# Four attention layers on one Trainium2 core: query stores held back, batch 0's queries loaded in two halves, stack loads moved by one step

## The chip, the cores and the metric

The kernel runs on one core of one Trainium2 chip. A core has five engines that run their own instruction streams: TensorE (PE in the profile, its weight loads PEld), VectorE (DVE), ScalarE (ACT), GpSimd (POOL) and SyncE (SP). They meet through semaphores. DMA transfers are issued from SP's queue and from POOL's queue and are carried out by 16 DMA engines. The metric is the device time of one launch in microseconds (us), as the median of several runs.

## The reference

The model has four layers on x of 8 batches x 256 tokens x 256 features. Each layer is a gated cross attention to a context of the same shape, and then a gated feed forward block (dense, two mixtures of experts, and a ternary one with a convolution). Only the attention is touched:

```python
h = layernorm(x)                                   # before each sublayer
q, k, v = h @ Wq + bq, ctx @ Wk + bk, ctx @ Wv + bv  # layer 0: h, ctx, ctx themselves
scores = einsum('bhqd,bhkd->bhqk', q, k) / sqrt(16)  # 16 heads of 16; layer 0 masked
out = einsum('bhqk,bhkd->bhqd', softmax(scores), v) @ Wo + bo
x = x + tanh(g_xattn[l]) * out
```

## The kernel before, in words

**Groups and batches.** The 2048 tokens are 4 groups of 512 tokens, so group g holds batches 2g and 2g+1. `project(l)` makes keys, values and queries of a layer group by group. TensorE multiplies, ScalarE writes the high part of the result (`q_hi`, `k_hi`), and VectorE writes the low part (`q_lo`, `k_lo`), the rest that a lower precision product needs. A group's queries are 1 MB: 512 KB high, 512 KB low.

**Through DRAM.** SP stores the parts into a DRAM tensor (`qk_parts`, by `store_k` and `store_q`), and POOL loads them back by batch into `stack`, which has 4 slots and holds heads in the layout that the scores need. `load_stack(l, b, at)` has four steps for a batch: `at` 0 and 1 are the keys of the two halves of the partitions, 2 and 3 the queries. Each step is two DMAs, of 128 KB (line 629) and of 256 KB (line 630). A small load of ones (line 622) comes with `at` 0 of the first four batches. `q_parts` has two buffers, so group 2 waits until group 0 is stored, and group 3 for group 1 (`stored(q_out, l, g - 2)`). The buffers of the keys lie in slot 3 of the stack.

**The attention loop.** `attend(l)` handles 256 (batch, head) units as 32 quads of 4 score pairs ("units" in this text: one PSUM bank, 2 matmuls at line 992). So a batch has 4 quads, and batch b begins at quad 4b. In quad n TensorE does, in this order: the scores of units 4n and 4n+1 (line 992) with the second scores, of units 13 earlier (line 996); a transpose of the maxima of quad n-1 (`max_rows`, line 1010); units 4n+2 and 4n+3; and the product with the values of quad n-4 (`times_v`, line 1037). VectorE takes the maximum of each unit (line 2092), ScalarE copies the transposed maxima (line 1526), and POOL writes them by DMA as a row into the stack (`put_rows`, line 667). The second scores of quad n need its row and are first due in quad n+3. ScalarE takes the exponentials (line 1517). At the first unit of a batch TensorE waits until every load of that batch has landed (`stack_in`):

```python
if c == 0 and h == 0:
    loads = sum(x % SLOTS == b % SLOTS for x in range(B)) * l + b // SLOTS + 1
    pe.wait_ge(stack_in[b % SLOTS], 128 * loads + 16 * (l + 1))
```

**POOL's order.** POOL issues the loads of batch 0, then three of the four steps of batch 1. Then it goes through the quads in order: wait for the row of quad n, put it, in quads 3 to 11 of layers 1 to 3 some work on the residual (line 644), and one step of a load:

```python
for n in range(QUADS):
    put_rows(l, n)
    ...
    if (n + 7) // 4 < B:
        load_stack(l, (n + 7) // 4, (n + 3) % 4)
```

In layer 0 it also makes the masks and takes the values between (lines 688 and 692). All of this is one queue in program order. At the first unit of a layer TensorE also waits for the low parts of all four groups of queries (line 964).

## Time and profile before

| | us |
|---|---|
| median of 3 runs | 1571.42 (1568.8 to 1572.77) |
| profiled execution, its own time | 1568.99 |
| its span | 1567.2 |
| TensorE busy | 1324.8 (85%) |
| VectorE busy | 962.4 (61%) |
| ScalarE busy | 860.1 (55%) |
| POOL busy | 708.6 (45%) |

The span is the time from the first to the last record of the profiled execution; its own time is 1.8 us more. Busy shares are means over stages with different limits, so they don't tell what bounds the stage that the change touches. "Idle before, releaser" in the rows is the time in which the engine did nothing just before an instruction, and what ended it. POOL's busy time does not count the waits of its queue.

### The profile page before, as it was taken

Reading aid. Unit: us, or ns where it says so; the run is one execution under the profiler, and the core shown is the slowest. Engines: PE = TensorE matmul, PEld = TensorE weight load, DVE = VectorE, ACT = ScalarE, POOL = GpSimd, SP = SyncE. Lnnn points to the kernel's source line nnn. Section 1 sums busy time; section 2 is a strip of 40 time slices with the busy share of each in tenths; the row PEclk is TensorE's granted clock in tenths of the full one; section 3 lists DMA queues with packets and bytes.
Section 4 is the critical chain, followed back from the end, with each engine's and each line's share of the span. In section 5 each row is a group of like instructions: output and inputs, shape, how many; then the busy total and the mean of one; then the engine's idle time right before and its main releaser. Section 6 shows DMA issues by size and latency. Waiting matters only on the chain.

```text
span 1567.2 us, 29388 instructions
## 1 busy us (share of the span) xinstructions
PE 1324.8 (85%) x9497; PEld 962.0 (61%) x9524; DVE 962.4 (61%) x2651; ACT 860.1 (55%) x1718; POOL 708.6 (45%) x835
## 2 busy tenths in 40 slices
PE   2899899997998499999999699849999388995985
PEld 1455489854566289999986366627887245664343
DVE  6789653426785643333338499575554277967787
ACT  2366854434786245555535388535554155885554
POOL 4567330105632577767641473158994415622000
PEclk9999999997899699999999699969999797997998
DMA  9997030179640333343248974024444498710001
GB/s 291 280 159 145 2 98 0 37 226 194 120 77 15 101 124 120 116 158 112 79 146 275 213 135 84 13 86 151 146 135 162 150 277 166 138 33 1 0 14 41
DMA packets 115441, 188.86 MB, mean 121 GB/s; under 512 B 21169, under 2 KB 91441, under 8 KB 109105
## 3 DMA queue, kind: packets, MB, share of 16 engines
q0 software_dynamic: 36928, 105.19, 28.2%
q1 hardware_dynamic: 78368, 81.79, 16.9%
q8 instruction: 86, 1.41, 0.4%
q14 instruction: 59, 0.48, 0.1%
HBM read 128.17 MB, written 50.20 MB: 114 GB/s over the span
## 4 chain that ended last, share of the span: by engine, by line
PE 67%; DVE 14%; DMA 7%; ACT 6%; issue 4%; POOL 1%; ACTq 0%; SPq 0%; DVEq 0%; POOLq 0%
PE PS L1196 10%; PE PS L1216 10%; PE PS L1037 9%; PE PS L992 8%; PE PS L996 3%; PE PS L1208 3%; PE PS L1074 2%; DMA qk_parts<-q_parts 2%; PE PS L1010 2%; PE PS L878 2%; PE PS L1050 2%; PE PS L1017 2%; DMA stack<-qk_parts 1%; DVE act L2577 1%; PE PS L864 1%
## 5 line engine op out<-in xcount | busy, mean ns | idle before, releaser
L2092 DVE TENSOR_REDUCE nm<-PS 128x2 f32<-128x512 f32 x384 | 250.3, 676 | 42.6 <-PE PS L992 41.4
L992 PE MATMUL PS<-stack 48*128 48x256 f32 x1024 | 215.8, 336 | 43.6 <-DVE nm L2092 10.6
L992 PEld LDWEIGHTS PS<-stack 48*128 48x128 f32 x1024 | 154.5, 208 | 128.5 <-issue 59.1
L996 PE MATMUL PS<-stack 49*128 49x256 f32 x1024 | 206.0, 325 | 0.9 <-ACT probs L1517 0.6
L1216 PE MATMUL PS<-weights,hh 128*128 x936 | 190.0, 292 | 3.9 <-DVE hl L2419 3.7
L1196 PE MATMUL PS<-weights,xh 128*128 x468 | 171.1, 420 | 10.7 <-DVE xl L2403 5.2
L667 POOL DMA_DIRECT2D stack<-mt x128 | 72.8, 569 | 213.8 <-ACT mt L1526 211.8
L1517 ACT ACTIVATE probs<-PS 128x512 f32<-128x512 f32 x256 | 145.1, 595 | 42.9 <-PE PS L996 16.7
L1517 ACT ACTIVATE xng<-PS 128x512 f32<-128x512 f32 x256 | 145.2, 595 | 24.3 <-PE PS L1017 13.8
L1216 PEld LDWEIGHTS PS<-weights,hh 128*128 128x128 f32 x936 | 152.8, 193 | 6.3 <-issue 5.8
L996 PEld LDWEIGHTS PS<-stack 49*128 49x128 f32 x1024 | 145.5, 198 | 10.1 <-ACT probs L1517 4.3
L1683 ACT ACTIVATE hh<-PS 128x512 fp32r<-128x512 f32 x117 | 65.7, 596 | 133.6 <-PE PS L1208 133.6
L1216 PE MATMUL PS<-weights,hl 128*128 x468 | 133.3, 285 | 0.0
L2088 DVE CUSTOM_DVE_ANT_0 PS<-PS,wslot 128x256 f32<-128x256 f32 x256 | 101.3, 449 | 19.9 <-PE PS L992 19.7
L1196 PEld LDWEIGHTS PS<-weights,xh 128*128 128x128 f32 x468 | 91.1, 195 | 36.0 <-issue 17.3
L629 POOL DMA_DIRECT2D stack<-qk_parts x128 | 64.0, 500 | 101.0 <-DMA qk_parts<-q_parts 67.1
L1673 ACT ACTIVATE PS<-bb 128x512 f32 x117 | 67.2, 596 | 52.3 <-issue 49.9
L1196 PE MATMUL PS<-weights,xl 128*128 x234 | 94.2, 403 | 0.0
L1216 PEld LDWEIGHTS PS<-weights,hl 128*128 128x128 f32 x468 | 90.8, 194 | 0.0
L771 POOL TENSOR_TENSOR weights<-weights 128x1024 fp32r<-128x1024 f32 (+1 forms) x48 | 88.6, 1846 | 2.5
L766 POOL TENSOR_TENSOR weights<-weights,zero 128x1024 fp32r<-128x1024 f32 (+1 forms) x48 | 70.7, 1472 | 32.2 <-DMA weights<-W_dram 31.8
L2419 DVE TENSOR_TENSOR hl<-PS,hh 128x512 fp32r<-128x512 f32 x117 | 76.5, 681 | 0.2 <-ACT hh L1683 0.2
(329 smaller groups left out, 3073.3 us busy)
## 6 DMA issues: line engine op xcount, KB each, us to landing
stack<-qk_parts POOLq DMA_DIRECT2D x128, 256.0 KB, 4.2
qk_parts<-stack SPq DMA_DIRECT2D x32, 512.0 KB, 6.9
qk_parts<-q_parts SPq DMA_DIRECT2D x32, 512.0 KB, 10.8
stack<-qk_parts POOLq DMA_DIRECT2D x128, 128.0 KB, 3.8
weights<-W_dram POOLq DMA_DIRECT2D x12, 1024.0 KB, 7.2
wide<-ctxT_dram SPq DMA_DIRECT2D x16, 512.0 KB, 8.1
wslot<-y_tokens SPq DMA_DIRECT2D x16, 512.0 KB, 7.6
weights<-W_dram POOLq DMA_DIRECT2D x12, 512.0 KB, 5.1
```

Of the source, the lines that this page charges most:

```text
L667: nc.gpsimd.dma_start(stack[MAXROW:MAXROW + 65:64, b % SLOTS, 0, c:c + 2, :].rearrange("p c n -> p (c n)"), mt[:, j % 4, :]).then_inc(row_ ...
L766: nc.gpsimd.tensor_tensor(wh, w, zero[:].broadcast_to([P, n // CUTS]), ALU.add).then_inc(split_hi, 1)
L771: ins = nc.gpsimd.tensor_tensor(wl, w, wh.bitcast(F32), ALU.subtract)
L992: mm = pe.matmul(PS[:, u % 3, to], nat_q[:, at], nat_k, start=True, stop=True)
L996: mm = pe.matmul(PS[:, 3 + v % 3, to], key_k[:, at], key_q, start=(l > 0 or half == 0), stop=(l > 0), skip_group_check=(l == 0))
L1037: mm = pe.matmul(PS[32 * strip:32 * strip + 32, 6, 0:S], vpad[:, 2 * b + kt, (DH + 1) * head:(DH + 1) * head + 32], probs_at(t, h)[:, kt * ...
L1196: add = lambda x, w: pe.matmul(PS[:, hid_bank(p) + h, :], x[:, p, c, :], w, start=False, stop=True, skip_group_check=True)
L1216: add = lambda x, w: pe.matmul(o, x, w, start=False, stop=True, skip_group_check=True)
L1517: nc.scalar.activation(probs_at(t, h), PS[:, 3 + v % 3, :], ACT.Exp, scale=SCALE).then_inc(exp_done, 1)
L2088: ins = nc.vector.tensor_tensor_reduce(ps, ps, mask_b[:, b, 0, row], -1.0, -MASKED * 4, ALU.add, ALU.min, nm[:, j % 2, at + qt:at + qt + 1])
L2092: nc.vector.tensor_reduce(nm[:, j % 2, at:at + 2], PS[:, (2 * t + h) % 3, :].rearrange("p (q n) -> p q n", q=2), AX.X, ALU.max, negate=Tru ...
L2419: nc.vector.tensor_tensor(hl[:, at].rearrange("p j t -> p (j t)"), PS[:, 3 + h, :], hh[:, at].rearrange("p j t -> p (j t)").bitcast(F32), ...
```

## The change

In layers 1 to 3 the queries of group 1 go into the space of `probs`, which the exponentials use later; so group 3 does not wait for the store of group 1. SP holds the stores back: group 1's begins when the first half of batch 0's loads has landed (`stack_first`), and the two stores of groups 2 and 3 each wait for one of the first four rows. Batch 0's queries come in two halves of four head pairs each, on two semaphores, in all layers; TensorE begins with the first half and waits for the second at unit 8. VectorE makes the low part of group 3 inside the attention loop, behind the first two maxima. TensorE waits for it before the transpose of quad 0's maxima, and ScalarE's first exponential waits until group 1 is stored. Only two steps of batch 1 are loaded ahead of the loop, so every later step of a load stands one quad later in POOL's queue.

```diff
-        def q_lo(g):
-            return q_parts[:, g % 2, 0]
-
-        def q_hi(g):
-            return q_parts[:, g % 2, 1]
+        def q_part(l, g, r):
+            if l and g == 1:
+                return probs[:].rearrange("p a n -> p (a n)").rearrange("p (r c n) -> p r c n", r=2, c=KC)[:, r].bitcast(F32R)
+            return q_parts[:, g % 2, r]
+        def q_lo(l, g):
+            return q_part(l, g, 0)
+        def q_hi(l, g):
+            return q_part(l, g, 1)
...
         k_out, q_out = sem("k_out", 2), sem("q_out", 2)
-        stack_in = sem("stack_in", SLOTS)
+        stack_in, stack_first = sem("stack_in", SLOTS), sem("stack_first")
...
+        def q_place(l, g):
+            return stored(q_out, l, g - 4 if l and g == 3 else g - 2)
...
                 sp.wait_ge(qlo_done, GROUPS * l + g + 1)
-                for r, part in enumerate((q_hi(g), q_lo(g))):
+                if l and g >= 2:
+                    sp.wait_ge(*stored(q_out, l, g - 2))
+                for r, part in enumerate((q_hi(l, g), q_lo(l, g))):
+                    if l and g == 1 and r == 0:
+                        sp.wait_ge(stack_first, 144 * (l + 1))
+                    if l and g >= 2:
+                        j = QUADS * l + 2 * (g - 2) + r
+                        sp.wait_ge(row_in[j % 4], 16 * (j // 4 + 1))
...
                     nc.gpsimd.dma_start(stack[MAXROW:MAXROW + 65:64, b % SLOTS, 1].rearrange("p c n -> p (c n)"),
-                                        io["ones_rows"]).then_inc(stack_in[b % SLOTS], 16)
+                                        io["ones_rows"]).then_inc(stack_in[b] if b else stack_first, 16)
                 pool.wait_ge(*stored((q_out, k_out)[of], l, b // 2))
...
                 first, both = (0, 1) if of else (2, 0)
-                nc.gpsimd.dma_start(rows(first, 1), part[0:DH]).then_inc(stack_in[b % SLOTS], 16)
-                nc.gpsimd.dma_start(rows(both, 2), part).then_inc(stack_in[b % SLOTS], 16)
+                landing = stack_in[b % SLOTS] if b else stack_first
+                nc.gpsimd.dma_start(rows(first, 1), part[0:DH]).then_inc(landing, 16)
+                nc.gpsimd.dma_start(rows(both, 2), part).then_inc(landing, 16)
+            def load_queries(l):
+                pool.wait_ge(*stored(q_out, l, 0))
+                for half in range(2):
+                    cs, landing = slice(PAIRS // 2 * half, PAIRS // 2 * (half + 1)), stack_in[0] if half else stack_first
+                    for h in range(2):
+                        rows = lambda r, n: stack[64 * h + DH * r:64 * h + DH * (r + n), 0, 0, cs].rearrange("p c n -> p (c n)")
+                        part = parts[0, 0, h, 0, :, cs].rearrange("p c n -> p (c n)")
+                        nc.gpsimd.dma_start(rows(2, 1), part[0:DH]).then_inc(landing, 16)
+                        nc.gpsimd.dma_start(rows(0, 2), part).then_inc(landing, 16)
...
                     make_mask(0)
-                    for at in range(4):
+                    for at in range(2):
                         load_stack(0, 0, at)
+                    load_queries(0)
                     make_mask(1)
                 else:
-                    for at in range(4):
+                    for at in range(2):
                         load_stack(l, 0, at)
-                for at in range(3):
+                    load_queries(l)
+                for at in range(2):
...
                         add_bo(l, n - 4)
-                    if (n + 7) // 4 < B:
-                        load_stack(l, (n + 7) // 4, (n + 3) % 4)
+                    if (n + 6) // 4 < B:
+                        load_stack(l, (n + 6) // 4, (n + 2) % 4)
...
                     if u == 0:
-                        pe.wait_ge(qlo_done, GROUPS * (l + 1))
+                        if l == 0:
+                            pe.wait_ge(qlo_done, GROUPS)
                         pe.wait_ge(klo_done, GROUPS * (l + 1))
...
                         loads = sum(x % SLOTS == b % SLOTS for x in range(B)) * l + b // SLOTS + 1
-                        pe.wait_ge(stack_in[b % SLOTS], 128 * loads + 16 * (l + 1))
+                        if b == 0:
+                            pe.wait_ge(stack_first, 144 * (l + 1))
+                        elif b % SLOTS:
+                            pe.wait_ge(stack_in[b % SLOTS], 128 * loads + 16 * (l + 1))
+                        else:
+                            pe.wait_ge(stack_in[0], 192 * (l + 1))
+                    if b == 0 and c == PAIRS // 2 and h == 0:
+                        pe.wait_ge(stack_in[0], 192 * l + 64)
...
                 pe.wait_ge(max_done, 4 * j + 4)
+                if l and n == 0:
+                    pe.wait_ge(qlo_done, GROUPS * (l + 1))
...
                 if l == 0 and g >= 2:
-                    act.wait_ge(*stored(q_out, l, g - 2))
+                    act.wait_ge(*q_place(l, g))
                 for c in range(KC):
-                    ins = nc.scalar.activation(xnT[:, c, at] if l else q_hi(g)[:, c], PS[:, xT_bank(2 * l, g) + c, :], ACT.Identity)
+                    ins = nc.scalar.activation(xnT[:, c, at] if l else q_hi(l, g)[:, c], PS[:, xT_bank(2 * l, g) + c, :], ACT.Identity)
                 ins.then_inc(xT_done if l else qhi_done, 1)
             def queries(l, g):
                 act.wait_ge(q_mm, GROUPS * (l - 1) + g + 1)
-                act.wait_ge(*stored(q_out, l, g - 2))
+                act.wait_ge(*q_place(l, g))
                 for oc in range(KC):
-                    ins = nc.scalar.activation(q_hi(g)[:, oc], PS[:, q_bank(l, g) + oc, :], ACT.Identity,
+                    ins = nc.scalar.activation(q_hi(l, g)[:, oc], PS[:, q_bank(l, g) + oc, :], ACT.Identity,
...
                 act.wait_ge(sc_mm, 2 * STEPS * l + v + 1)
+                if l and v == 0:
+                    act.wait_ge(*stored(q_out, l, 1))
...
                 if l or g >= 2:
-                    dve.wait_ge(*stored(q_out, l, g - 2))
+                    dve.wait_ge(*q_place(l, g))
                 if l == 0:
-                    nc.vector.tensor_tensor(q_lo(g), PS[:, 2 * g:2 * g + 2, :], q_hi(g).bitcast(F32), ALU.subtract
+                    nc.vector.tensor_tensor(q_lo(l, g), PS[:, 2 * g:2 * g + 2, :], q_hi(l, g).bitcast(F32), ALU.subtract
                                             ).then_inc(qlo_done, 1)
...
                     ins = nc.vector.scalar_tensor_tensor(
-                        q_lo(g)[:, oc], PS[:, q_bank(l, g) + oc, :], col(f"bq{l}", oc) if l != 2 else 0.0,
-                        q_hi(g)[:, oc].bitcast(F32), ALU.add, ALU.subtract)
+                        q_lo(l, g)[:, oc], PS[:, q_bank(l, g) + oc, :], col(f"bq{l}", oc) if l != 2 else 0.0,
+                        q_hi(l, g)[:, oc].bitcast(F32), ALU.add, ALU.subtract)
...
                             layernorm(l, 2 * l, g + 2)
-                        queries(l, g)
+                        if g + 1 < GROUPS:
+                            queries(l, g)
...
                         maximum(l, 2 * n, 1)
+                    if l and n == 0:
+                        queries(l, GROUPS - 1)
...
                 queries(l + 1, 2)
-                queries(l + 1, 3)
```

## Rows read from the trace of the kernel before

**Rows 1.** The page: busy time, share of the span and instructions.
```profile
PE 1324.8 (85%) x9497; PEld 962.0 (61%) x9524; DVE 962.4 (61%) x2651; ACT 860.1 (55%) x1718; POOL 708.6 (45%) x835
```
**Rows 2.** The chain that ended last, layer 1's start: start us, length us, what.
```profile
353.34 0.49 POOL stack L629
...
354.78 8.35 DMA stack<-qk_parts
...
363.37 0.82 PE PS L992 x4
```
**Rows 3.** The chain that ended last, start of layer 2.
```profile
856.11 13.76 DMA qk_parts<-q_parts
...
872.07 5.75 PE PS L904 x8
...
880.31 0.56 PE PS L992 x4
```
**Rows 4.** The chain that ended last, start of layer 3.
```profile
1286.92 3.71 PE PS L904 x8
...
1293.47 0.53 PE PS L992 x4
...
1299.29 6.18 DMA stack<-qk_parts
```
**Rows 5.** Timeline, starts of layers 1 and 3: start, length, instruction, [idle before <-releaser].
```profile
350.82 7.03 PE L904 MATMUL PS<-wide,wproj 128*128 128x512 f32 x16
...
359.94 1.41 DVE L2031 SCALAR_TENSOR_TENSOR q_parts<-PS,cols,q_parts 128x512 fp32r<-128x512 f32 x2 [2.77 <-ACT q_parts L1462]
...
1293.98 6.30 DVE L2092 TENSOR_REDUCE nm<-PS 128x2 f32<-128x512 f32 x10 [0.61 <-PE PS L992]
```
**Rows 6.** Timeline of POOL in layer 2: quad 17's row and load.
```profile
938.63 0.57 POOL L667 DMA_DIRECT2D stack<-mt  x1 [1.39 <-ACT mt L1526]
...
939.68 0.51 POOL L630 DMA_DIRECT2D stack<-qk_parts  x1
```
**Rows 7.** Timeline of TensorE in layer 2: the first matmuls of quads 18 and 20.
```profile
936.55 0.38 PE L992 MATMUL PS<-stack 48*128 48x256 f32 x1
...
942.42 0.38 PE L992 MATMUL PS<-stack 48*128 48x256 f32 x1
```
**Rows 8.** Line 630 from 940 to 964 us: issues, and issue to landing.
```profile
L630 POOL DMA_DIRECT2D stack<-qk_parts x8: 505/505/507, 939.7 to 960.2; - x8
...
DMA to landing us min/median/max: 3.1/3.9/4.0
```
**Rows 9.** Line 630 from 904 to 917 us, layer 2, quads 5 to 9.
```profile
L630 POOL DMA_DIRECT2D stack<-qk_parts x5: 506/511/518, 904.3 to 916.6; - x5
...
DMA to landing us min/median/max: 3.8/4.1/5.3
```
**Rows 10.** Timeline of TensorE, layer 2: first matmuls of quads 8 and 12, two waits behind.
```profile
905.21 0.38 PE L992 MATMUL PS<-stack 48*128 48x256 f32 x1
...
909.64 0.35 PE L992 MATMUL PS<-stack 48*128 48x256 f32 x1 [0.99 <-DVE nm L2092]
...
918.09 0.38 PE L992 MATMUL PS<-stack 48*128 48x256 f32 x1
...
922.21 0.35 PE L992 MATMUL PS<-stack 48*128 48x256 f32 x1 [0.66 <-issue]
```
**Rows 11.** Line 630 from 93 to 108 us, layer 0, quads 9 to 13.
```profile
L630 POOL DMA_DIRECT2D stack<-qk_parts x5: 495/497/498, 93.1 to 107.3; - x5
...
DMA to landing us min/median/max: 3.9/5.9/6.6
```
**Rows 12.** Timeline of TensorE, layer 0: quad 12's second pair, quad 16's first matmul.
```profile
96.23 0.35 PE L992 MATMUL PS<-stack 48*128 48x256 f32 x1 [0.27 <-issue]
...
111.64 0.38 PE L992 MATMUL PS<-stack 48*128 48x256 f32 x1 [0.32 <-DMA stack<-qk_parts]
```
**Rows 13.** Busy time of engines, granted clock (third from the end), DMA share, GB/s: layer 1.
```profile
396.00:404.00 8.00, 8.00 (x58) 4.74 (x61) 5.18 (x11) 4.39 (x10) 4.80 (x7) 0.50 0.50 79
```

## The prediction

> **What bounds the kernel now.** I read the page first, then the chain that ended last at the start of each layer's attention, then the timelines of POOL, VectorE and TensorE inside the attention, and last, for single loads, the time from issue to landing. The page says that TensorE is busy for 85% of the span, more than any other engine [rows 1]. So work or waits on TensorE count nearly in full, unless a transfer sets the end.
>
> There are two stages. At the start of an attention TensorE stands still. In layer 1 it waits for the loads of batch 0: POOL begins to issue the queries at 353.34, the last load takes 8.35 us, and the first scores start at 363.37 [rows 2]. In layers 2 and 3 it waits for group 3's low part: its own projection is over at 877.82 and 1290.63, its scores start at 880.31 and 1293.47 [rows 3, 4]. Inside the attention TensorE runs without a gap: two quads take 942.42 - 936.55 = 5.87 us, or 2.94 each [rows 7]. There nothing waits for loads. That is the cover which one part of this change uses up.
>
> **The start of layers 1 to 3.** The change removes the competition of the stores of groups 1 to 3, halves what TensorE waits for, and takes group 3's low part off its way.
>
> - Layer 1: POOL issues the four DMAs of the first half from 353.34 to about 355.3 [rows 2]. I take 3.1 to 4.0 us for the last landing, as for loads at a quiet time [rows 8], less a little because they are half as long. TensorE's own projection ends at 357.85 [rows 5]. So it begins at about 358.5 in place of 363.4: 4.9 us gained.
> - Layer 2: the store of group 0 takes 13.76 us [rows 3]. Group 1's store stands behind it in SP's queue, so holding that back does not speed it up. The start moves from 880.31 to the end of the projection, 872.07 + 5.75 = 877.82: 2.5 us.
> - Layer 3: from 1293.47 to 1286.92 + 3.71 = 1290.63: 2.8 us [rows 4].
> - What it costs: two instructions of together 1.41 us (1.3 in layer 2) now stand between VectorE's maxima [rows 5]. Ten maxima take 6.30 us with no gap at this place [rows 5], so VectorE is what TensorE waits for, and nothing covers them: 1.4, 1.3 and 1.4 us.
>
> Net: -(4.9 + 2.5 + 2.8) + 4.1 = -6.1 us. TensorE's granted clock could also stay up where the gap goes. From 396 to 404 us it was 0.50, that is 1.2 GHz, behind a gap in TensorE's work, and TensorE was busy for all 8 us [rows 13]: that is up to 4 us lost. I give this nothing in the sum, and up to 8 us over three layers in the range.
>
> **New waits at the start.** Group 1's store now begins when TensorE does. ScalarE's first exponential waits for it, some 10 us later (14 maxima of 0.63 us and the 1.4 us). The store of a group took 13.76 us where much else was under way [rows 3], and after the change less is. I take it as just hidden. The stores of groups 2 and 3 wait for rows that come anyway; SP has nothing urgent behind them.
>
> **All loads one quad later.** This is the part that decides. POOL's queue is in order. A step of a load stands behind the row of its quad, and that row exists only when the next quad has begun. In the pattern of layer 2, the row of quad 17 is put at 938.63, which is 2.08 us after quad 18 begins at 936.55, and the second DMA of the load is issued at 939.68, 3.13 us after it [rows 6, 7]. Its like land 3.9 us after issue (median of 8) [rows 8]. So a load behind row n has landed 7.03 us after quad n+1 begins.
>
> Before, the last load of batch b stands behind row 4b-4. TensorE needs it at quad 4b, three quads after quad 4b-3 begins: 3 x 2.94 = 8.81 us, a margin of 1.8 us. After the change it stands behind row 4b-3 and has two quads: 5.87 us. It is late by 7.03 - 5.87 = 1.16 us. TensorE's first unit of the batch waits, and VectorE, ScalarE and the next rows wait behind it. No engine catches up, for TensorE has no gaps in which to do so [rows 7].
>
> - Batches 4 to 7 of layers 1 to 3: 12 x 1.15 = 13.8 us.
> - Batches 2 and 3 are later still, because POOL's work on the residual (line 644) stands in between. In layer 2 the loads in the place in question are issued at 904.3 (903.8 without the ones, by one issue of 0.5 us as in [rows 6]) and 916.6 and land after 4.1 to 5.3; I take 4.7 [rows 9]. They are needed at 905.21 and 918.09 [rows 10]: late by 3.3 and 3.2. Of this 0.99 and 0.66 replace waits that are there before [rows 10]: 2.3 + 2.5 = 4.8 us. In layer 1 quads 9 to 11 run at 1.2 GHz [rows 13] and give batch 3 its time: 2.3. Layer 3 I take at the mean, 3.5. Together 10.6 us.
> - Batch 1 of layers 1 to 3: in layer 3 its last load is issued at 1299.29, 5.8 us after the start, and lands at 1305.47, 12.0 after it [rows 4]. After the change the issue comes 1.4 later, for the low part, and four maxima (2.5 us) later: 9.7, and lands at 13.6 to 15.9 with 3.9 [rows 8] to 6.18 us. It is needed at 12.0 + 1.4 = 13.4. Late by 0.2 to 2.5; I take 0.9, nearer to the low end because the stores that stretched it are held back: 2.7 us.
> - Layer 0: the quads are longer, but POOL also makes masks and the loads land after 5.9 us (median) [rows 11]. The load behind row 9 is issued at 93.1 and lands at 99.0, needed at 96.2; that behind row 13 at 107.3 + 5.9 = 113.2, needed at 111.64 [rows 11, 12]. Late by 2.8 and 1.6, on average 2.2, for batches 1 to 4: 8.8 us. The last three have enough time, since masks no longer delay POOL.
>
> **The sum.** -6.1 + 13.8 + 10.6 + 2.7 + 8.8 = +29.8 us. The profiled execution's span of 1567.2 becomes 1597.0, and its own time, 1.8 more, 1598.8. That execution was 2.4 us under the median of the runs. Against the median: 1571.4 + 29.8 = 1601 us.
>
> Low bounds: every quiet load lands in 3.1 us, the least in [rows 8], so 0.4 us late in place of 1.15 (-9); layer 0 only half as late (-4.4); the clock stays up at two starts (-5): 1583. High bounds: the longer stalls drop the clock in layers 0, 2 and 3 (+4 each, [rows 13]), loads of batches 2 and 3 land after 5.3 in place of 4.7 us (+4): 1617.
>
> **The rivals.**
>
> *The loads are hidden anyway (the other side).* If the last load of a batch landed within 5.87 - 3.13 = 2.74 us of its issue, the shift would cost nothing in the steady part, and the gains at the start would remain. With batches 1 to 3 also in time this gives 1571.4 - 6.1 = 1565 us. Against it: none of the eight loads in [rows 8] landed within 3.1 us. For it: the loads follow each other with less in between, and some landings are short. The Trainium skill, "DMA: Bandwidth & Descriptors", section on the anatomy of one DMA, gives about 2.0 us plus the bytes over 436 GB/s for a POOL DMA, 2.6 us for 256 KB. By that rule the steady part costs nothing and the sum is 1601 - 13.8 = 1587. The trace does not agree: 3.9 us with the smaller load just ahead of it [rows 8]. Chance 0.06.
>
> *The shift is half hidden.* Landings near 3.1 us, and the clock kept up at the starts, with layer 0's waits lost in POOL's other waits. The stalls of about 15 us stand against gains of 6 to 12: about 1576, from 1567 to 1583. For it: TensorE's clock was down after each late start. Against it: the maxima keep TensorE half idle in the first ten microseconds with or without the gap. Chance 0.10.
>
> *The stalls cost the clock as well.* Batches 2 and 3 wait for 3 us, and the quads behind them run at 1.2 GHz as in [rows 13]. With six such stalls at up to 4 us, 1617 to 1630. The Trainium skill, "TensorE: Matmul & The Clock Gate", section on HAM oscillation, says that waits for DMA throttle TensorE again; the trace agrees, with 0.50 at 396 to 404 us. Against it: at half clock the next batch has more time, so the second stall shrinks, as layer 1's batch 3. Chance 0.08.
>
> **How the numbers follow.** Forecast 0.76: 1583 to 1617, likeliest 1601. The others as above. The range 1583 to 1618 leaves out the first two rivals and most of the third. A measurement of this kernel can tell about 0.3%, 4.7 us, from no change. The first rival is faster (0.06). Of the second about 0.04 lies within 4.7 us of 1571.4 and 0.01 below. Faster 0.07, same 0.04, slower 0.89.
>
> **What would show it.** Right: at the first unit of batches 2 to 7 TensorE waits for DMA stack<-qk_parts, by 1 to 3 us, six times in a layer; the twelve steady ones by 1.1 us each. The starts come at about 5, 2.5 and 3 us less behind the projection, with a maximum chain interrupted by 1.4 us at line 2031's place. SP's stores of groups 2 and 3 come behind rows. Wrong: quads 16, 20, 24 and 28 follow without a gap; or ScalarE's first exponential or the rows wait for the held stores; or the gap at layer 2's start is gone because the store of group 0 became shorter than 13.76 us.

## The result, and the profile after

The changed kernel takes 1616.0 us (median of 4 runs, 1612.96 to 1621.73), beside 1572.1 us of the kernel before in the same comparison: ratio 1.0279, 95% interval 1.0255 to 1.0302. It is slower by 44 us; 1601 was forecast, in a range from 1583 to 1618. The profiled execution has a span of 1619.9 us and an own time of 1621.73, so it lies 5.7 us above the median; its span is 52.7 us longer than that of before.

From the page of the kernel after: its engines, the shares of the chain that ended last, and the groups of VectorE's maxima and of TensorE's scores. The numbers behind the bar are busy us and mean ns of one, then the idle time before them, who ended most of it, and how much of it that one ended:

```profile
PE 1344.7 (83%) x9524; PEld 969.5 (60%) x9524; DVE 961.7 (59%) x2651; ACT 860.4 (53%) x1718; POOL 718.7 (44%) x851
...
PE 58%; DVE 13%; DMA 13%; ACT 6%; issue 5%; POOL 4%; SPq 1%; ACTq 0%; DVEq 0%; POOLq 0%
PE PS L1257 10%; PE PS L1237 10%; DMA stack<-qk_parts 8%; PE PS L1031 6%; PE PS L1078 6%; PE PS L1249 3%; PE PS L1115 2%; DMA qk_parts<-q_parts 2%; PE PS L1035 2%; PE PS L1058 1%; PE PS L1051 1%; PE PS L1091 1%; DVE act L2622 1%; PE PS L909 1%; PE PS L1183 1%
...
L2136 DVE TENSOR_REDUCE nm<-PS 128x2 f32<-128x512 f32 x384 | 249.7, 676 | 94.2 <-PE PS L1031 94.0
L1031 PE MATMUL PS<-stack 48*128 48x256 f32 x1024 | 222.5, 346 | 78.3 <-DMA stack<-qk_parts 55.9
```

TensorE is still the engine that is busiest, but it now idles 78.3 us ahead of the scores (line 1031), and 55.9 us of that ends with a load of the stack. The loads are 8% of the chain that ended last. VectorE's maxima wait 94.0 us for those scores. TensorE's busy time is also 19.9 us longer than in [rows 1], for the same work: part of it ran at a lower clock. (Some 4 us of the difference can be records that the trace of before lacks: it has 9497 matmuls and that of after 9524, at 0.14 us each.)

Where the waits are. The timeline of TensorE in the kernel after, first the matmuls that waited for a load in layer 0 (batches 1, 2, 3 and 5), then those of layer 1 (batches 1 to 7):

```profile
59.93 0.58 PE L1031 MATMUL PS<-stack 48*128 48x256 f32 x1 [3.30 <-DMA stack<-qk_parts]
84.87 0.58 PE L1031 MATMUL PS<-stack 48*128 48x256 f32 x1 [5.61 <-DMA stack<-qk_parts]
108.00 0.58 PE L1031 MATMUL PS<-stack 48*128 48x256 f32 x1 [4.88 <-DMA stack<-qk_parts]
145.18 0.38 PE L1031 MATMUL PS<-stack 48*128 48x256 f32 x1 [3.25 <-DMA stack<-qk_parts]
...
389.05 0.58 PE L1031 MATMUL PS<-stack 48*128 48x256 f32 x1 [5.27 <-DMA stack<-qk_parts]
405.54 0.57 PE L1031 MATMUL PS<-stack 48*128 48x256 f32 x1 [2.42 <-DMA stack<-qk_parts]
422.57 0.55 PE L1031 MATMUL PS<-stack 48*128 48x256 f32 x1 [2.46 <-DMA stack<-qk_parts]
438.28 0.38 PE L1031 MATMUL PS<-stack 48*128 48x256 f32 x1 [1.12 <-DMA stack<-qk_parts]
451.35 0.38 PE L1031 MATMUL PS<-stack 48*128 48x256 f32 x1 [1.24 <-DMA stack<-qk_parts]
465.71 0.38 PE L1031 MATMUL PS<-stack 48*128 48x256 f32 x1 [1.11 <-DMA stack<-qk_parts]
478.53 0.38 PE L1031 MATMUL PS<-stack 48*128 48x256 f32 x1 [1.00 <-DMA stack<-qk_parts]
```

Layers 2 and 3 show the same pattern: batch 1 waits 3.31 and 3.15 us, batches 2 and 3 together 3.26 and 4.39, batches 4 to 7 from 0.97 to 1.46 each. Summed over the kernel: layer 0 17.0 us, batch 1 of layers 1 to 3 11.7, batches 2 and 3 12.5, the twelve steady ones 14.2, together 55.4. The kernel before waits for a load at two of these 28 places, 0.32 us at batch 4 of layer 0 [rows 12] and 0.27 us at batch 1 of layer 3.

One steady wait, step by step. The timelines of TensorE and POOL around batch 5 of layer 1, and for line 648 in this place the time from issue to landing:

```profile
446.24 0.57 POOL L696 DMA_DIRECT2D stack<-mt  x1 [1.39 <-ACT mt L1569]
...
447.10 0.38 PE L1031 MATMUL PS<-stack 48*128 48x256 f32 x1
...
447.29 0.51 POOL L648 DMA_DIRECT2D stack<-qk_parts  x1
```

```profile
L648 POOL DMA_DIRECT2D stack<-qk_parts x1: 512/512/512, 447.3 to 447.3; - x1
...
DMA to landing us min/median/max: 4.0/4.0/4.0
```

The quad ahead began at 444.16 (2.94 us before the one at 447.10), the load is issued 3.13 us after that, behind the row, and lands 4.0 us later, at about 451.3. The batch would be next at 447.10 + 2.94 = 450.04. TensorE begins it at 451.35, behind a wait of 1.24 us. That is the sum of the prediction, with the same numbers as in [rows 6 to 8].

The starts. The chain that ended last at layer 1's start, and the timeline of TensorE at the starts of layers 2 and 3 (projection, then first scores):

```profile
363.00 4.07 DMA qk_parts<-q_parts
...
367.35 0.49 POOL stack L658
...
368.79 3.22 DMA stack<-qk_parts
372.01 0.24 issue
372.25 0.53 PE PS L1031 x4
```

```profile
894.94 6.45 PE L935 MATMUL PS<-wide,wproj 128*128 128x512 f32 x8 [11.17 <-ACT wide L1495]
901.32 0.73 PE L1031 MATMUL PS<-stack 48*128 48x256 f32 x6
...
1324.05 5.24 PE L935 MATMUL PS<-wide,wproj 128*128 128x512 f32 x8 [2.92 <-ACT wide L1495]
1329.21 0.73 PE L1031 MATMUL PS<-stack 48*128 48x256 f32 x6
```

In layer 1 the first half is issued from 367.35 and its last load takes 3.22 us, where it was 8.35 [rows 2]; the scores start 4.9 us after the first issue in place of 10.0. In layers 2 and 3 they follow the projection without a gap, as forecast. The wait just ahead of the first scores falls from 5.52, 2.50 and 2.85 us to 0.41, 0 and 0, so by 5.1, 2.5 and 2.9 (4.9, 2.5 and 2.8 were forecast). From the end of the previous attention to the first scores it is 6.8, 1.8 and 2.2 us less than before. VectorE pays for it with the late low part, here in layer 1:

```profile
372.76 1.29 DVE L2136 TENSOR_REDUCE nm<-PS 128x2 f32<-128x512 f32 x2 [1.61 <-PE PS L1031]
373.97 1.40 DVE L2074 SCALAR_TENSOR_TENSOR q_parts<-PS,cols,q_parts 128x512 fp32r<-128x512 f32 x2
375.28 2.47 DVE L2136 TENSOR_REDUCE nm<-PS 128x2 f32<-128x512 f32 x4
```

From the first scores to the end of the last product with V the attentions take 169.0, 128.4, 124.7 and 129.0 us, beside 154.1, 114.5, 107.8 and 111.7 before: 14.9, 13.9, 16.9 and 17.3 us more, 63 in all. In layers 0 and 1 that is less than their waits for loads (17.0 and 14.6 us), since some of these stand where TensorE waited for something else before. In layers 2 and 3 it is more (11.2 and 12.6 us). The clock has a part in that: over an attention the mean granted clock falls from 0.967, 0.877, 0.937 and 0.908 to 0.929, 0.854, 0.863 and 0.841. Busy time by windows in layer 1 of the kernel after (columns as in [rows 13], the granted clock is the third from the end):

```profile
372.00:382.00 10.00, 7.51 (x32) 5.11 (x32) 8.80 (x15) 2.81 (x5) 3.97 (x9) 0.64 0.92 215
382.00:392.00 10.00, 4.73 (x34) 3.35 (x34) 4.30 (x7) 3.73 (x10) 3.56 (x7) 0.50 1.11 246
...
442.00:452.00 10.00, 8.61 (x105) 5.53 (x105) 8.13 (x19) 7.73 (x19) 4.66 (x9) 1.00 0.78 150
452.00:462.00 10.00, 9.89 (x105) 6.25 (x105) 8.28 (x18) 7.74 (x18) 4.38 (x9) 0.83 0.49 92
```

In the last window TensorE is busy for 9.89 us and still does no more matmuls than in the window with a wait, since part of it ran at 1.2 GHz.

### The profile page after: what moved, and what is told of

It is laid out like the page before. It is cut to its first block, busy times and chain, and to the rows that moved or that the text cites. A ratio compares the mean times of both kernels' runs of the same rounds, so it can differ in the third digit from the quotient of the medians.

```text
span 1619.9 us, 29444 instructions
## 1 busy us (share of the span) xinstructions
PE 1344.7 (83%) x9524; PEld 969.5 (60%) x9524; DVE 961.7 (59%) x2651; ACT 860.4 (53%) x1718; POOL 718.7 (44%) x851
## 4 chain that ended last, share of the span: by engine, by line
PE 58%; DVE 13%; DMA 13%; ACT 6%; issue 5%; POOL 4%; SPq 1%; ACTq 0%; DVEq 0%; POOLq 0%
PE PS L1257 10%; PE PS L1237 10%; DMA stack<-qk_parts 8%; PE PS L1031 6%; PE PS L1078 6%; PE PS L1249 3%; PE PS L1115 2%; DMA qk_parts<-q_parts 2%; PE PS L1035 2%; PE PS L1058 1%; PE PS L1051 1%; PE PS L1091 1%; DVE act L2622 1%; PE PS L909 1%; PE PS L1183 1%
## 5 line engine op out<-in xcount | busy, mean ns | idle before, releaser
L1031 PE MATMUL PS<-stack 48*128 48x256 f32 x1024 | 222.5, 346 | 78.3 <-DMA stack<-qk_parts 55.9
L1031 PEld LDWEIGHTS PS<-stack 48*128 48x128 f32 x1024 | 161.0, 218 | 167.5 <-DMA stack<-qk_parts 68.3
L1035 PE MATMUL PS<-stack 49*128 49x256 f32 x1024 | 212.5, 336 | 0.9 <-ACT probs L1560 0.6
L1035 PEld LDWEIGHTS PS<-stack 49*128 49x128 f32 x1024 | 152.5, 209 | 10.1 <-ACT probs L1560 4.8
L1078 PE MATMUL PS<-probs,vpad 128*32 128x256 f32 x1024 | 80.6, 438 | 2.2 <-ACT mt L1569 0.7
```

The lines of the kernel that those rows point to most:

```text
L1031: mm = pe.matmul(PS[:, u % 3, to], nat_q[:, at], nat_k, start=True, stop=True)
L1035: mm = pe.matmul(PS[:, 3 + v % 3, to], key_k[:, at], key_q, start=(l > 0 or half == 0), stop=(l > 0), skip_group_check=(l == 0))
L1078: mm = pe.matmul(PS[32 * strip:32 * strip + 32, 6, 0:S], vpad[:, 2 * b + kt, (DH + 1) * head:(DH + 1) * head + 32], probs_at(t, h)[:, kt * ...
```

## The experiments

The change has two kinds of parts: the order of the loads on one side; held stores, halves and the late low part on the other. All differences below are of the ratios to the kernel before, times 1568 us, its median on these chips (1567.96, 1568.74 and 1568.34 in three sets of runs).

**The order of the loads undone, all else kept.**

```diff
-                for at in range(2):
+                for at in range(3):
                     load_stack(l, 1, at)
...
-                    if (n + 6) // 4 < B:
-                        load_stack(l, (n + 6) // 4, (n + 2) % 4)
+                    if (n + 7) // 4 < B:
+                        load_stack(l, (n + 7) // 4, (n + 3) % 4)
```

> The kernel after, with the loads of batches 1 to 7 in the order of the kernel before again: three steps of a batch's load ahead of the first rows, and n + 7 in the loop. The held stores, the halves of batch 0's queries and the late low part stay. Theory (the whole loss is the shift of the loads by one quad): TensorE's waits for DMA stack<-qk_parts at the first unit of batches 1 to 7, 55 us together after the change, are gone, and the gains at the starts stay, so about 1572 - 6 = 1566 us, from 1560 to 1572. Rival (the held stores and the halves themselves starve the loads of batch 1 and the clock falls at the starts): the waits at batch 1, 12 us in layers 1 to 3, and the slower clock behind the starts stay, and the time is over 1580 us.

Measured: 1558.45 us, ratio 0.9913 (0.9884 to 0.9942), and once more, on another chip, with this expectation:

> The kernel after with the order of the loads of before once more, as the base of the other two on the same chip, in five rounds. Theory: the gain of the first time (0.9913, from 0.9884 to 0.9942) is there again: 0.989 to 0.994. Rival (part of it was the scatter of that chip): 0.994 to 0.998, as the held stores or the halves alone.

1556.51 us, 0.9918 (0.9891 to 0.9946). Of the 55 us of waits, 1.3 us are left in the four layers of the first trace. The theory holds for the waits, and its time was too high: 1558 us lies below its 1560 to 1572. Without the shift the kernel is 13 us faster than before, twice the 6 us that I had.

**The shift alone, in the kernel before.** The same lines changed the other way.

> The kernel before with the shift alone: two steps of a batch's load ahead of the first rows in place of three, and n + 6 in the loop in place of n + 7. Nothing else is changed. Theory (the shift is all of the loss): TensorE waits at the first unit of batches 1 to 7 as in the kernel after, 14 us in the twelve steady ones, 12 us at batches 2 and 3 of layers 1 to 3, and 17 us in layer 0, and the time is that after plus the gains at the starts that are missing, 1616 + 6 = 1622 us, from 1610 to 1628. Rival (the loss comes from the shift together with the held stores at batch 1): batch 1 of layers 1 to 3 waits for under 1 us and the time is about 1572 + 14 + 12 + 9 = 1607 us. If the shift is harmless: 1572.

Measured: 1633.02 us, ratio 1.0413 (1.038 to 1.0446), 65 us slower, beyond the upper end of the theory (1628). The steady waits are there, 15.1 us in twelve; batches 2 and 3 of layers 1 to 3 wait 15.9. Batch 1 waits 2.05, 1.93 and 3.79 us, so the rival is refuted: it waits without the held stores too, in layers 1 and 2 less than in the kernel after (5.27 and 3.31) and in layer 3 more (3.15). The other parts of the change go with 1.3 us more at batch 1 on average; which of them was not tried. They gain 21 us with the shift (1.0413 to 1.0279) and 13 without it, a difference of about the size of the intervals.

**One step earlier than before.** As the first one, with `range(4)` and `n + 8`.

> The kernel after with the loads two quads earlier, that is one quad earlier than in the kernel before: all four steps of batch 1 ahead of the first rows, and n + 8 in the loop. Theory (a load behind row n lands 7 us after the next quad begins, and what is not needed earlier gains nothing): with three quads of time the margin was 1.8 us, with four it is 4.7 us; so the steady batches gain nothing over the kernel with the order of before, and batches 1 to 3 of each layer, whose loads come late behind other work of POOL, gain what they still wait for, some 2 to 5 us in all: about 1563 us. Rival (the loads ahead of the rows hold up the first rows, and these hold up the maxima and the exponentials): the first rows of an attention come 1 to 2 us later and the time is 1570 to 1576 us. A wait of a load for the scores that still read its slot would show in POOL's waits.

Measured: 1563.4 us, ratio 0.9965 (0.9946 to 0.9985), 8 us slower than with the order of before. The 1563 us of the theory are met by accident: it reckoned with a base of 1566 and a gain of 3. Against the base that was measured the rival is right, with one thing in it wrong: the rows are not issued later, they land later. Line 696, the first row of layer 1, from issue to landing, first in this kernel and then with the order of before:

```profile
L696 POOL DMA_DIRECT2D stack<-mt x1: 570/570/570, 366.5 to 366.5; - x1
...
DMA to landing us min/median/max: 8.9/8.9/8.9
```

```profile
L696 POOL DMA_DIRECT2D stack<-mt x1: 575/575/575, 367.2 to 367.2; - x1
...
DMA to landing us min/median/max: 4.0/4.0/4.0
```

In layers 2 and 3 the first row takes 6.5 and 6.3 us here, and 2.4 to 5.6 in the two traces with the order of before. TensorE needs the row for the second scores of quad 0. Its timeline in this kernel shows it standing still until 0.1 us behind the landing (366.46 + 8.9 = 375.3):

```profile
375.43 0.55 PE L1031 MATMUL PS<-stack 48*128 48x256 f32 x1 [5.47 <-issue]
```

And what ScalarE does there in this kernel (its timeline):

```profile
372.22 1.28 ACT L1560 ACT_TABLE_LOAD   x1 [3.35 <-DMA qk_parts<-probs]
376.26 0.60 ACT L1560 ACTIVATE probs<-PS 128x512 f32<-128x512 f32 x1 [2.76 <-PE PS L1035]
```

ScalarE waits 3.35 us for the held store of group 1, until 372.22. That costs nothing here: behind its table load it waits 2.76 us more, for the second scores, so the row is what it waited for last. The first product with V comes 19.5, 16.8 and 17.1 us behind the first scores in layers 1 to 3, in place of 16.8, 14.8 and 14.3: 7.5 us. So both directions cost something: a step later makes the batches wait, a step earlier delays the landing of the first rows.

**The low part ahead of the attention again, with the order of before.** The two `queries(l + 1, 3)` and `queries(l, g)` lines go back, and the scores wait for the low part at unit 0.

> The kernel after with the order of the loads of before and, beside it, group 3's low part made ahead of the attention as in the kernel before; held stores and halves stay. Against the kernel with only the order undone this prices the late low part. Theory: TensorE's scores start 2.5 us later in layers 2 and 3, where the low part is last, and not in layer 1, and 1.4 us of VectorE's work leave the row of maxima in each layer: 5 us against 4.1 us, so 0 to 2 us slower than that kernel, about 1567. Rival (the starts are hidden behind VectorE's row of maxima anyway, so only when the maxima end counts): no difference, or up to 4 us faster.

Measured: 1557.57 us, ratio 0.9926 (0.9897 to 0.9956), against 0.9913 and 0.9918. No difference that these runs can tell; between a cost of 2 us and nothing it stays open. (The 1567 us of the theory started from 1566 again.) One thing in the theory is wrong: the low part is last in layer 1 too. TensorE's first scores wait for it 2.80, 2.50 and 2.80 us in this trace. So the late low part saves about 8 us at the starts, and since the times are equal about as much must be lost again. The attentions of layers 1 to 3 are 3 and 7 us shorter here than in the two traces with the late low part.

**The held stores alone, and the halves alone.** Both from the last kernel, and both keep group 1's queries in `probs`, so group 3 does not wait for the store of group 1. Without halves, batch 0 is loaded with `load_stack(l, 0, at)` for four steps. Without held stores, these lines go:

```diff
-                    if l and g == 1 and r == 0:
-                        sp.wait_ge(stack_first, 144 * (l + 1))
-                    if l and g >= 2:
-                        j = QUADS * l + 2 * (g - 2) + r
-                        sp.wait_ge(row_in[j % 4], 16 * (j // 4 + 1))
```

> The kernel before with the held stores alone: the stores of groups 1 to 3 wait as in the kernel after (group 1's for all of batch 0's load, since there are no halves; its parts lie in probs, as in after). Queries of batch 0 in one piece, low part of group 3 ahead of the attention, loads in the order of before. Theory A (the competition of the stores with the loads is what delays the first scores and the first quads): most of the 14 us that the kernel after gains with the order undone, so about 1559 us. Theory B (the halves are what counts, since TensorE waits for half as many loads): under 4 us gained, 1564 to 1568.

> The kernel before with the halves of batch 0's queries alone: the stores of groups 1 to 3 go out as soon as their parts are made, as before; the parts of group 1 still lie in probs. Low part ahead, loads in the order of before. Theory A (the stores' competition is what counts): under 4 us gained, 1564 to 1568 us. Theory B (the halves count): layer 1's start comes 3 to 5 us earlier and the time is about 1560 us; layers 2 and 3 start after the low part in either case and gain nothing.

Measured: held alone 1561.47 us, 0.9951 (0.9924 to 0.9978); halves alone 1562.81 us, 0.9955 (0.9928 to 0.9981). Neither theory: each kernel is 7 to 8 us faster than before, with both parts it is 12 (0.9926). All three gains contain group 1's new place. If the parts simply added up, the held stores would bring 4 to 5 us, the halves 4, and the new place 3; with intervals of 4 us on each ratio this is no more than a rival to "7 us each". The new place alone was not run.

**The shift in layer 0 alone.** From the kernel with the order of before: `range(3 if l else 2)` and `step = n + (7 if l else 6)`.

> The kernel after with the order of the loads of before in layers 1 to 3 and its own, one quad later, in layer 0 alone. It prices the shift in layer 0, which I had at 8.8 us and where the trace of after shows 17 us of waits at batches 1, 2, 3 and 5. Theory (a wait costs what it is long, since TensorE has no gap to catch up in): 12 to 17 us over the kernel with the order undone everywhere (0.9913 of before), so 1570 to 1576 us, and layers 1 to 3 take as long as there. Rival (the waits are absorbed, as layer 0's quads are longer and TensorE can be ahead): 3 to 9 us, so 1561 to 1567 us.

Measured: 1565.09 us, ratio 0.9971 (0.9942 to 1.0), so 8 to 9 us over the base, though its trace has 13.8 us of waits in layer 0. The rival is nearer. A reason is in the trace of the kernel with the order of before everywhere: TensorE already stands still in the same quad there, 8, as its timeline shows. The row of quad 5, which its second scores need, was put late, behind the making of a mask on POOL, and took 5.6 us, so it landed at 79.5:

```profile
79.61 0.55 PE L1031 MATMUL PS<-stack 48*128 48x256 f32 x1 [4.67 <-issue]
```

```profile
73.91 0.61 POOL L696 DMA_DIRECT2D stack<-mt  x1
```

In the kernel after TensorE waits 5.61 us for the load at the first matmul of that quad (84.87), and the row of quad 5 lands meanwhile, at 82.7. So by these two traces only 0.94 us of it is new: 3.30 + 0.94 + 4.88 + 3.25 = 12.4 of 17.0, and layer 0's attention is 12.1 us longer in the kernel after than in this one. The second trace of the kernel with the order of before has it 5 us longer than the first (162.0 and 156.9), so single traces settle this to some 5 us only.

**Batch 1 in time, batches 2 to 7 a step late.** From the kernel after: `range(3)`, and in the loop

```diff
+                    step = n + 6 if n else 7
+                    if n != 1 and step // 4 < B:
+                        load_stack(l, step // 4, step % 4)
```

> The kernel after, with batch 1's loads in the places that they have in the kernel before (three steps ahead of the first rows, the fourth behind row 0), and batches 2 to 7 one quad later as in after. It prices batch 1, which I had at 2.7 us in layers 1 to 3 and where the trace of after shows 11.7 us of waits, and 3.3 in layer 0. Theory (the waits at batch 1 cost their length and the half clock behind them): 12 to 20 us under the kernel after (1.028 of before), so 1592 to 1602 us; the twelve steady waits of 1.2 us stay as they are. Rival (with batch 1 in time, batch 2's loads have less time by as much, so the wait only moves on): batch 2's waits grow from 2 to 5 us each and the time is 1604 to 1612 us.

Measured: 1609.47 us, ratio 1.0251 (1.0192 to 1.031), against 1.0279: the theory's 12 to 20 us are not there, and the interval is too wide to say more than that batch 1 is worth less than about 15 us. The waits at batch 1 are gone in all layers, yet layer 1's attention takes 127.0 us in place of 128.4. The time is the rival's, but not for its reason: batch 2 waits 2.55, 2.23 and 0.51 us in place of 2.42, 0.44 and 2.12, 5.3 us in place of 5.0. The product with V of quad 0 comes 2.5 to 3.6 us sooner in each of layers 1 to 3, and layer 2 gives that back with quads at half clock later (30.7 us from the product with V of quad 8 to that of quad 16 in place of 27.1). In layer 1 another wait takes the place of the 5.27 us: TensorE stands still for 2.96 us inside quad 3 until the row of quad 0 lands. So a wait this early is partly one for the first row under another name.

**The steady batches alone, one and two quads late.** From the kernel with the order of before, batches 4 to 7 of layers 1 to 3:

```diff
-                    if (n + 7) // 4 < B:
-                        load_stack(l, (n + 7) // 4, (n + 3) % 4)
+                    for step in range(7, 4 * B):
+                        if n == step - (7 if step < 16 or l == 0 else 6):
+                            load_stack(l, step // 4, step % 4)
```

and 5 in place of 6 for two.

> The kernel after with the order of the loads of before, but with the loads of batches 4 to 7 of layers 1 to 3 one quad later, as after has them. It prices the steady part alone, which I had at 13.8 us. Theory (a load behind row n lands 7 us after the next quad begins and is needed 5.9 after it): twelve waits of 1.2 us, 14.4 us over the kernel with the order undone (1558), and 3 to 6 us more for the quads that run at half clock behind some of the waits, so 1573 to 1579 us. Rival (the waits of 1.2 us come only where earlier stalls had put POOL and TensorE out of step; with batches 1 to 3 in time the load lands in time): no waits, 1558 to 1562 us.

> The same as the kernel with the steady part one quad late, but two quads late: the last load of batches 4 to 7 of layers 1 to 3 stands behind row 4b-2 and has one quad. Theory (the time of a wait is 7.0 us less the quads that are left): 7.0 - 2.9 = 4.1 us at each of the twelve batches, 49 us over the kernel with the order undone, so 1607 us, and up to 12 quads at half clock behind them, 2 us each: 1607 to 1631. Rival (with the quads stretched by the waits, the row comes no later but the landing is faster, since less is moved at a time): waits of under 3 us and 1585 to 1600 us.

Measured: one late 1575.08 us, 1.0043 (1.0017 to 1.0069); two late 1635.39 us, 1.0454 (1.0394 to 1.0514). Against 0.9918 that is 19.6 us (with 6 of uncertainty) and 84 (with 10). One late lies in the range of its theory. Two late lies above its own (1607 to 1631), though the waits come as it said. TensorE's timeline with the steady part one late, three batches of layer 1:

```profile
431.26 0.38 PE L1032 MATMUL PS<-stack 48*128 48x256 f32 x1 [1.13 <-DMA stack<-qk_parts]
444.39 0.38 PE L1032 MATMUL PS<-stack 48*128 48x256 f32 x1 [1.31 <-DMA stack<-qk_parts]
457.52 0.38 PE L1032 MATMUL PS<-stack 48*128 48x256 f32 x1 [1.30 <-DMA stack<-qk_parts]
```

Twelve such waits sum to 15.9 us. This profiled execution took 1584.21 us, 9 above the median of its runs. Two late, the timelines of POOL and TensorE at one batch, and the busy time by windows around it:

```profile
431.32 0.49 POOL L648 DMA_DIRECT2D stack<-qk_parts  x1
...
435.29 0.58 PE L1032 MATMUL PS<-stack 48*128 48x256 f32 x1 [4.10 <-DMA stack<-qk_parts]
```

```profile
431.00:435.00 4.00, 0.19 (x4) 0.00 (x0) 0.48 (x1) 0.38 (x1) 0.81 (x2) 0.78 0.58 99
435.00:437.00 2.00, 1.71 (x11) 1.43 (x11) 0.88 (x2) 0.85 (x2) 0.00 (x0) 0.50 0.00 0
437.00:439.00 2.00, 2.00 (x18) 1.27 (x20) 1.49 (x5) 1.24 (x4) 1.34 (x3) 0.50 0.05 10
439.00:441.00 2.00, 2.00 (x25) 0.91 (x18) 0.84 (x2) 0.82 (x3) 0.22 (x1) 0.73 0.91 193
441.00:443.00 2.00, 1.95 (x27) 1.22 (x27) 2.00 (x6) 2.00 (x5) 0.70 (x2) 1.00 0.08 4
```

Twelve waits from 3.70 to 4.16 us, 4.00 on average, where the arithmetic gave 4.1: with one quad less, a wait is a quad longer. But the waits sum to 48.0 us and the kernel loses 84. Behind this wait the clock is granted at 0.50, 1.2 GHz, for about 4 us, while TensorE is busy. From 2 to 4 us behind the end of the wait it is 0.50 at all twelve. The quad ahead of the batch, the wait and the batch's first quad take 12.0 us together at this place where 2 x 2.94 + 4.1 = 10.0 would do. Over the twelve, from the quad ahead of a batch to its third, 28 us go beyond the quads at 2.94 and the waits, so waits and slower quads make 76 us; the remaining 8 lie within the interval. The three stretches of batches 4 to 7 run at a granted clock of 0.76, 0.83 and 0.84, where it is 1.00 with the order of before.

## Why the prediction was right, and where it was off

The sign, the place and the mechanism were right, and the time lies in the range, 15 us above the likeliest value and 2 below the upper end. Two parts of the sum were too small, with opposite signs. The sum had -6.1 for the starts and +35.9 for the shift; the runs give -13 and +57 (0.9913 to 1.0279), together +44. That the misses of 7 and 21 us partly cancel is luck: with the shift sized right and the starts as they stand the forecast would have been 1623, above its own range.

*The starts, -6.1.* They came as forecast, step by step, in the traces of the kernel after: 3.22 us for the last load of a half, the projection's end as the start in layers 2 and 3, 1.40 us for the low part. But the term was mis-sized: without the shift the change gains 13 us. The gaps ahead of the starts of layers 1 to 3 are 11.4 and 10.9 us shorter than before in the two traces without the shift, where I had 10.2. So the -10.2 is right, and what did not show is the +4.1 for the low part: the attentions of layers 1 to 3 together are 2.7 us shorter in one trace and 1.4 longer in the other. A likely reason, not tested by itself, is in the trace of before: inside quad 3 TensorE waits for the row of quad 0 in each of these layers, 1.57, 1.34 and 1.77 us. Without the shift it waits there in layer 1 alone in one trace (2.69 us) and in layers 1 and 3 in the other (3.04 and 2.27), so the time of quad 3 goes by when the row lands and not by the maxima alone. In layer 3 of before the row is put at 1298.24 and takes 4.6 us, and this wait ends just behind, though the profile names VectorE:

```profile
1302.90 0.55 PE L992 MATMUL PS<-stack 48*128 48x256 f32 x1 [1.77 <-DVE nm L2092]
```

The clock, which I gave nothing in the sum and up to 8 us in the range, carries part of it in layer 1. There a row that landed late was followed by quads of 5.8, 5.0 and 4.0 us before, and now there is one of 3.9; the mean granted clock of this attention is 0.877 before, and 0.923 and 0.924 in the two traces. How the rest divides is below what single profiled executions tell.

*Batches 4 to 7, 13.8.* The waits measure 14.2 us in the kernel after and 15.9 where they stand alone. The term is right for the wait. Its price is 19.6 us, and with 6 us of uncertainty that can't be told from 15.9.

The Trainium skill, "DMA: Bandwidth & Descriptors", section on the anatomy of one DMA, gives 2.6 us for the 256 KB as an estimate, and by it the steady part costs nothing. The kernel after shows 4.0 us for it behind the 128 KB of its step, and the runs show the waits; the measurement decides against the rule here.

*Batches 2 and 3 (10.6) and batch 1 (2.7) of layers 1 to 3.* The waits are 12.5 and 11.7 us. The cost of the shift outside the steady part and layer 0 is 57.4 - 19.6 - 8.7 = 29.1 us (with some 10 of uncertainty), where I had 13.3. Batch 1 is the step that failed by most: I took its load as 0.9 us late, and it was 3.9 late on average. The part that was wrong in all three layers is when TensorE needs it. I had 12.0 + 1.4 = 13.4 us after the start, and it is ready for it after 11.5, 11.4 and 11.2. The 12.0 held a wait for the row of quad 0, shown above for layer 3 of before. With one step of loads fewer ahead of it and the stores held back this row lands in 3.5, 1.7 and 1.7 us in the kernel after, in place of 5.0, 4.7 and 4.6, and that wait is gone, which also swallows the 1.4 us. The landing was about right: 14.7 and 14.4 us after the start in layers 2 and 3, in the 13.6 to 15.9 that I had. In layer 1 it was 16.8: the last load was issued at 382.39, 10.1 us after the start (9.7 was forecast), and took 6.6 us, above my upper end of 6.18. The ground that held stores leave batch 1 free is not borne out, for with the shift alone and no held stores it was 2.6 late. The experiment with batch 1 in time could not say how much of the 29 us is batch 1's.

*Layer 0, 8.8.* The price is right, 8 to 9 us (with some 6 of uncertainty), for a partly wrong reason, so part of it is luck: the waits are 13.8 to 17.0 us, not 8.8, and not all of their length counts, as one replaces a wait that was there. The working also took the second pair of quad 12, at 96.23, for the moment when batch 3 needs its load; its first matmul began at 95.46, so that load was 3.5 us late by this working and not 2.8. And batch 5, which I had in time, waited 3.25 us in the kernel after.

*"I give this nothing": the clock.* This is the other term that was mis-sized, at nothing. I counted a wait at its length. In the kernel after quads of up to 5.0 us in place of 2.94 follow the longer waits. The third rival, stalls that cost the clock as well (1617 to 1630), describes what happened better, though the time stayed just below it, since the starts gained more. The kernel with the steady part two quads late shows the cause: the same work at the same place, only the waits longer, the granted clock 0.50 behind each of the twelve, and 84 us lost for 48 of waits. For waits of about 1.2 us it is not shown that they cost more than their length on the whole. Among the twelve of the kernel after the clock fell behind three, of 1.24, 1.35 and 1.46 us, each with 1.3 to 1.5 us lost over the next quads, and stayed at 1.00 behind nine, of 0.97 to 1.31 us.

The Trainium skill, "TensorE: Matmul & The Clock Gate", section on HAM oscillation, says that waits for DMA throttle TensorE again; these traces agree for every wait of about 4 us (0.50 behind all twelve), and for three of twelve waits of about 1.2 us in the kernel after.

*New waits at the start.* ScalarE's wait for group 1's store was taken as just hidden: it is 0.64 us in layer 1 of the kernel after and nothing in layers 2 and 3. It was near the edge: in the kernel with the loads one step earlier it is 3.35 us in layer 1, though there ScalarE then waits for the second scores as well.

*The first two rivals.* Loads hidden anyway is refuted by the steady waits, 12 of 12 in each trace with the shift in these batches. Half hidden (1567 to 1583) is refuted by the time.

## What to carry to other kernels

For a load that stands in an in-order queue behind a product of the pipeline, work out two numbers in units of the pipeline's step: when it lands after the step that releases it begins (here 7.0 us), and how many steps are left (3 x 2.94, 2 x 2.94, 1 x 2.94 gave no wait, 1.2 us and 4.0 us). A wait of the bounding engine can cost more than its length, because its clock can fall behind it: here 1.75 times for waits of 4 us; for 1.2 us these runs can't tell the price from the length. When a wait is measured in the kernel before, ask what else TensorE waited for ahead of it, and whether the change moves that too: here the row of quad 0. And a change with parts of both signs is worth taking apart: with the shift undone, the other parts made this kernel 0.8% faster than before, where the whole made it 2.8% slower.

## What the runs showed of the hardware that was not expected

- A wait of 1.2 to 1.5 us is enough for a lower clock at times, and its length does not decide it alone. In the kernel with the steady part one late the clock fell behind waits of 1.28, 1.67 and 2.21 us and stayed at 1.00 behind others of up to 1.51. Where it fell behind a wait of the kernel after, the next quad took 3.7 to 3.8 us at a full clock's 2.94. Behind each of the twelve waits of about 4 us the granted clock was 0.50.
- How long the 4 KB row of quad 0 takes to land goes with what else is under way. In layers 1 to 3, in nine traces of kernels with held stores and halves, it took 1.7 to 3.5 us with up to two of POOL's loads not yet landed when it was issued, 2.7 to 6.0 with three or four, and 5.6 to 8.9 with five or six. With the shift alone in the kernel before, where the stores are not held, it took 3.2 to 5.2 us behind no load or one. A small row on the path of the maxima pays for large transfers around it, though its issue is not held up.
